# An eight-core kernel's first stage: seven of eight batches summed on TensorE, the eighth scaled on ScalarE, and two groups of instructions moved in their queues

## The chip, the cores and the metric

One Trainium2 chip, all 8 cores. Every core runs the same program on the same kind of data, with no exchange between them. The metric is the device time of the slowest core, in microseconds (us). A core has five engines with queues of their own, worked off in order: TensorE (PE, matmuls), VectorE (DVE), ScalarE (ACT), GpSimd (POOL) and SyncE (SP, which here issues transfers). They are held together only by semaphores.

## The reference

The program is a chain of four layers on x of 8 batches, 2048 tokens and 1024 features: a retention-like attention, a routed feed-forward, a delta-rule block and the routed feed-forward again. The change touches only the first one:

```python
def _L0_attn_a_ref(x, Wq, Wk, Wv):        # x: layer norm of the input
    Q = jnp.einsum('bti,id->btd', x, Wq)
    K = jnp.einsum('bti,id->btd', x, Wk)
    V = jnp.einsum('bti,id->btd', x, Wv)
    m = jnp.einsum('btd,bt->td', K, V.sum(axis=-1))
    ...
    return S[None, :, :] * Q              # S: decayed running sum of m over t
```

V's sum over its features is the product of the normed x with one vector, the row sums of Wv. So m is (sum over the 8 batches of c[b,t] * xhat[b,t,:]) times Wk, where c is a number per batch and token. The kernel works this out from the raw x: y = sum over b of coef[b,t] * x[b,t,:] plus a mean term, and then one product with Wk. Q is wanted for one batch only, the core's own (batch 0 of its data).

## The kernel before

**Tiles.** The tokens form NT = 16 tiles of 128. For each token tile `tt` there are B = 8 tiles of 128 tokens x 1024 features, f32, one a batch, numbered n = 8 tt + b. Four of them are a group gi (NGRP = 32 groups; group 2 tt has batches 0 to 3, group 2 tt + 1 has 4 to 7), and two are a unit (NUNIT = 64), which is what one transfer brings. They lie in `ring`, 16 slots, two token tiles deep.

**What each engine does in the first stage**, token tile by token tile:

- SP (L347 to L356) issues the units' transfers. Before it refills a slot it waits until PE has summed the old unit (`a_ymm`), and for a unit with batch 0 also until the own tile has been normed (`a_ownln`).
- ACT (`stats`, L401) takes sum and sum of squares of the tiles of six batches, three a group, in two passes each; `own_norm` (L417) makes the normed own tile `ownln`; `q_evict` (L428) copies Q from PSUM (`qps`) into `x_tok`. Order in a turn: `stats(2tt)`, `stats(2tt+1)`, `q_evict(tt-1)`, `own_norm(tt)`.
- DVE (`tiles`, L542) multiplies each tile by the vector of Wv's sums and adds up (`dotw`), and takes the statistics of batches 0 and 4; `coefs` (L557) makes four coefficients and signals `a_coef`; `mean_term` (L571); `own_evict` (L578) copies the transposed own tile to `ownfm`; `y_finish` (L584) adds the mean term to the sum in PSUM (`yps`) and writes `y16`; `y_evict` (L594) copies the transposed y to `y_fm`. Order in a turn: `tiles(2tt)`, `coefs(2tt)`, `own_evict(tt-1)`, `y_finish(tt-1)`, `tiles(2tt+1)`, `y_evict(tt-1)`, `coefs(2tt+1)`, `mean_term(tt)`.
- POOL (L368 to L375) makes, out of each coefficient column, a diagonal 128x128 matrix (`diag`, 8 places), and signals `a_diag` for each.
- PE (`y_rows`, L470) multiplies each tile by its diagonal, in two halves of 512 columns, and adds up the 8 batches in PSUM. An f32 product shows as two records in the trace, so a tile has four and a token tile 32. `own_project` (L483) first transposes `ownln` (8 small products, `trq`), waits for DVE's copy `ownfm`, and multiplies it by Wq (16 products, `qps`); `y_transpose` (L504) transposes `y16`. Order in a turn: `y_rows(2tt-1)`, `own_project(tt-1)`, `y_transpose(tt-1)`, `y_rows(2tt)`.

`yps` has two buffers, `qps` and the transposes' targets one each. The order on every engine is written out by hand. Behind the last Q product (`a_qmm` = 16) POOL loads Wk into the place of Wq, and PE multiplies y by it (L530): the second part of this layer. The rest of the program follows.

## Time and profile before

| | us |
|---|---|
| median of 3 runs (1994.53 to 1999.36) | 1994.77 |
| the profiled execution, slowest core | 1988.95 |
| its span (core 1, first to last instruction) | 1986.4 |
| spans of the eight cores | 1970.3 to 1986.4 |
| PE busy over the span | 1687.0 (85%) |
| DVE busy | 885.1 (45%) |
| ACT busy | 691.1 (35%) |
| POOL busy | 196.4 (10%) |

The rows below are of one execution and of its slowest core, core 1. Its first stage runs from the start to about 361 us. Times are from the core's first instruction. "Idle before" tells how long the engine had nothing to do ahead of a row, and what ended it. PE rows are merged runs of products; the end of the last one of a run is modelled, so the start-to-start time is the better measure.

### The profile page before, as it was taken

To read this page: it belongs to the slowest core of one execution; us is meant where nothing else is said; L and a number is where in the kernel's file an instruction comes from. 1 tells how busy PE (TensorE), PEld (TensorE's weight loads), DVE (VectorE), ACT (ScalarE), POOL (GpSimd) and SP (SyncE) were. 2 spreads that over 40 slices of the span, in tenths; PEclk is the share of its full clock that TensorE was granted. 3 is DMA by queue.
4 is the path that set the end of the run, shared out by engine and by line. 5 is a ranking of instruction groups with operands and counts; after the bars stand their busy time and mean duration, and the time that the engine had idled before them with its cause. 6 is when DMAs were issued, how large, how long until landed. Compare 5 with 4: busy or idle time off the path is not lost.

```text
span 1986.4 us, 23643 instructions; the slowest of 8 cores (1970.3 to 1986.4 us)
## 1 busy us (share of the span) xinstructions
PE 1687.0 (85%) x8330; PEld 801.6 (40%) x8330; DVE 885.1 (45%) x1699; ACT 691.1 (35%) x1051; POOL 196.4 (10%) x272
## 2 busy tenths in 40 slices
PE   1999999681399996898999999999999995289997
PEld 0444444230244442444554444444444442144443
DVE  3788888387421115436442432442222346611222
ACT  4788887047412223410323221340001110722112
POOL 2212121020301004000000000000000000300002
PEclk8999999895599997999999999999999998589999
DMA  9776773385227729920010010571044322173445
GB/s 277 217 233 203 221 217 123 66 147 105 86 43 128 127 53 205 246 48 1 1 44 22 22 43 1 104 135 27 1 70 85 58 43 53 43 233 64 85 85 85
DMA packets 69425, 201.14 MB, mean 101 GB/s; under 512 B 4606, under 2 KB 4670, under 8 KB 69312
## 3 DMA queue, kind: packets, MB, share of 16 engines
q0 software_dynamic: 40960, 94.76, 26.7%
q1 hardware_dynamic: 28352, 104.88, 16.5%
q8 instruction: 69, 1.13, 0.2%
q14 instruction: 44, 0.36, 0.1%
HBM read 228.97 MB, written 33.59 MB: 132 GB/s over the span
## 4 chain that ended last, share of the span: by engine, by line
PE 78%; DMA 7%; DVE 7%; issue 4%; ACT 2%; DVEq 1%; POOL 0%; ACTq 0%; another core or an unknown queue 0%; SPq 0%; POOLq 0%
PE v_h1ps L971 11%; PE v_h2ps L983 10%; PE yps L478 10%; PE mlp_a L1653 6%; PE mlp_a L1641 5%; PE ab_bank L1488 5%; PE ab_bank L1526 3%; PE mlp_a L1667 3%; PE ab_bank L1439 3%; PE mlp_r L1667 3%; PE ab_big L1413 3%; PE qps L499 3%; PE ab_bank L1432 3%; PE ab_bank L1382 3%; PE ab_bank L1501 2%
## 5 line engine op out<-in xcount | busy, mean ns | idle before, releaser
L478 PE MATMUL yps<-ring,diag 128*128 128x512 f32 x512 | 225.9, 599 | 12.1 <-POOL diag L374 12.1
L971 PE MATMUL v_h1ps<-m_sel_fm,m_w 128*128 128x512 bf16 x1024 | 222.5, 379 | 0.0
L983 PE MATMUL v_h2ps<-m_w,m_h1q 128*128 128x512 bf16 x1024 | 222.3, 379 | 0.0
L918 ACT ACTIVATE m_h1q<-v_h1ps,fb_s 128x512 bf16<-128x512 f32 x128 | 87.8, 687 | 294.4 <-PE v_h1ps L971 294.4
L891 DVE TENSOR_TENSOR m_acc<-v_h2ps,m_acc 128x512 f32<-128x512 f32 x96 | 66.3, 691 | 262.0 <-PE v_h2ps L983 262.0
L547 DVE SCALAR_TENSOR_TENSOR scr_v<-ring,wvs_bc 128x1024 bf16<-128x1024 f32 x128 | 152.6, 1211 | 0.6 <-issue 0.6
L971 PEld LDWEIGHTS v_h1ps<-m_sel_fm,m_w 128*128 128x128 bf16 x1024 | 100.3, 98 | 120.4 <-issue 0.3
L983 PEld LDWEIGHTS v_h2ps<-m_w,m_h1q 128*128 128x128 bf16 x1024 | 100.1, 98 | 120.9
L478 PEld LDWEIGHTS yps<-ring,diag 128*128 128x128 f32 x512 | 96.9, 192 | 128.8 <-issue 128.8
L1625 ACT ACTIVATE gate_prod<-mlp_a 128x512 bf16<-128x512 f32 x64 | 38.2, 597 | 273.8 <-PE mlp_a L1641 273.6
L1641 PE MATMUL mlp_a<-xln_fm,wg_buf 128*128 128x512 bf16 x512 | 113.8, 383 | 2.6 <-ACT gate_prod L1625 2.6
L1653 PE MATMUL mlp_a<-xln_fm,wu_buf 128*128 128x512 bf16 x512 | 111.8, 379 | 0.0
L413 ACT ACTIVATE scr_s<-ring,a_mv 128x1024 bf16<-128x1024 f32 x96 | 109.2, 1138 | 2.2
L1595 DVE TENSOR_TENSOR gate_prod<-mlp_a,gate_prod 128x512 bf16<-128x512 f32 x64 | 44.3, 692 | 135.7 <-PE mlp_a L1653 135.6
L408 ACT ACTIVATE scr_s<-ring 128x1024 bf16<-128x1024 f32 x96 | 100.3, 1046 | 7.2 <-DMA ring<-x_all 2.6
L374 POOL TENSOR_SCALAR diag<-cs_ident,a_coef 128x128 f32<-128x128 f32 x128 | 61.9, 501 | 249.2 <-DVE a_coef L567 244.1
L530 PE MATMUL mps<-y_fm,wk 128*128 128x512 bf16 x256 | 57.9, 387 | 26.7 <-DMA wk<-aWk 18.5
L1641 PEld LDWEIGHTS mlp_a<-xln_fm,wg_buf 128*128 128x128 bf16 x512 | 50.3, 99 | 64.8 <-issue 5.9
L1653 PEld LDWEIGHTS mlp_a<-xln_fm,wu_buf 128*128 128x128 bf16 x512 | 50.0, 98 | 60.2 <-issue 0.3
L1488 PE MATMUL ab_bank<-q_fm,k_fm 128*128 128x512 bf16 (+3 forms) x320 | 65.3, 347 | 9.5 <-DVE x_tok L1246 4.0
L499 PE MATMUL qps<-wq,ownfm 128*128 128x512 bf16 x256 | 57.8, 379 | 17.9 <-DVE ownfm L582 15.2
L1667 PE MATMUL mlp_a<-wd_buf,gate_prod 128*128 128x512 bf16 x256 | 60.4, 379 | 9.2 <-DVE gate_prod L1595 9.2
(263 smaller groups left out, 2251.4 us busy)
## 6 DMA issues: line engine op xcount, KB each, us to landing
ring<-x_all SPq DMA_DIRECT2D x64, 1024.0 KB, 6.8
m_w<-fW POOLq DMA_DIRECT2D x16, 2048.0 KB, 14.4
x_tok<-x_all POOLq DMA_DIRECT2D x16, 512.0 KB, 7.8
y_dram<-x_tok SPq DMA_DIRECT2D x4, 2048.0 KB, 26.6
x_tok<-y_dram SPq DMA_DIRECT2D x16, 512.0 KB, 4.4
x_tok<-y_dram POOLq DMA_DIRECT2D x16, 512.0 KB, 6.0
out<-x_tok SPq DMA_DIRECT2D x4, 2048.0 KB, 21.1
m_sel_tok<-sel_dram SPq DMA_DIRECT2D x8, 514.0 KB, 6.0
```

The lines of the kernel that those rows point to most:

```text
L408: s.activation(out=scr_s[:, q * D:(q + 1) * D], in_=x_tile(n), func=AF.Identity, scale=1.0 / (32.0 * D), accum_out=mv[:, 2 * n:2 * n + 1])
L413: ii = s.activation(out=scr_s[:, q * D:(q + 1) * D], in_=x_tile(n), func=AF.Square, scale=-1.0 / 32.0, bias=mv[:, 2 * n:2 * n + 1], accum_ ...
L478: ii = t.matmul(yps[tt % 2][:, h * 512:(h + 1) * 512], lhsT=diag_of(n), rhs=x_tile(n)[:, h * 512:(h + 1) * 512], start=(n % B == 0), stop= ...
L499: ii = t.matmul(qps[:, h * 512:(h + 1) * 512], lhsT=ownfm[:, dt * P:(dt + 1) * P], rhs=wq16[:, dt * D + h * 512:dt * D + (h + 1) * 512], s ...
L547: v.scalar_tensor_tensor(out=scr_v[:, j % 2 * D:(j % 2 + 1) * D], in0=x_tile(n), scalar=1.0, in1=wvs_bc[:, :], op0=ALU.mult, op1=ALU.mult, ...
L918: s.activation(out=h1q[:, ft * D + h * 512:ft * D + (h + 1) * 512], in_=h1ps[n % 4][:, :], func=AF.Gelu_apprx_tanh, bias=fb1_s[:, q * 8 + ...
L971: ii = t.matmul(h1ps[n % 4][:, :], lhsT=w1[:, dt * D + ft * P:dt * D + (ft + 1) * P], rhs=sel_fm[:, dt * D + h * 512:dt * D + (h + 1) * 51 ...
L983: ii = t.matmul(h2ps[m % 4][:, :], lhsT=h1q[:, ff * D + rt * P:ff * D + (rt + 1) * P], rhs=w2[:, ff * D + h * 512:ff * D + (h + 1) * 512], ...
L1488: ii = t.matmul(dst[:, lo:512], lhsT=fm_tile(k_fm, j, dt), rhs=fm_sb(src, I, dt, lo), start=dt == 0, stop=dt == ND - 1)
L1641: ii = t.matmul(psA[ft % 2][:, 0:512], lhsT=wg_buf[:, dt * D + ft * P:dt * D + (ft + 1) * P], rhs=xfm16[:, dt * T + tb * 512:dt * T + (tb ...
L1653: ii = t.matmul(psA[2 + ft % 2][:, 0:512], lhsT=wu_buf[:, dt * D + ft * P:dt * D + (ft + 1) * P], rhs=xfm16[:, dt * T + tb * 512:dt * T + ...
L1667: ii = t.matmul(dst, lhsT=prod_t[:, ff * 512 + ttl * P:ff * 512 + (ttl + 1) * P], rhs=wd_buf[:, ff * D + nh * 512:ff * D + (nh + 1) * 512] ...
```

## The change

PE sums only the first NPE = 7 batches of a token tile. The tile of the eighth is multiplied by its coefficient on ACT (`z_scale`), into a place of `x_tok` that is not in use yet (`z_of`: the last two token tiles' places in turn), and DVE's `y_finish` adds it while it adds the mean term. POOL makes seven diagonals a token tile instead of eight. The signals are counted anew (`diag_no`, `ymm_no`): there are still four `a_ymm` signals a token tile, the last one behind the single batch 6.

`own_project` is split: the transposes (`own_transpose(tt-1)`) stay behind `y_rows(2tt-1)`, the products with Wq and `y_transpose(tt-1)` go behind `y_rows(2tt)`. On ACT `q_evict` moves by a turn, to `q_evict(tt-2)` behind `stats(2tt)` and `z_scale(tt-1)`. On DVE `y_evict(tt-1)` goes behind `coefs(2tt+1)` and `mean_term(tt)`. SP's refill of a unit with batches 6 and 7 also waits for `a_z`, and the last two `q_evict` wait for `a_ysum`.

```diff
@@ -29,6 +29,8 @@
 NGRP = 2 * NT
 NUNIT = 4 * NT
 NSLOT = 8
+
+NPE = 7
 
 def build_consts():
     c = {}
...
@@ -335,6 +338,15 @@
         def unit_of(n):
             return n // 2
 
+        def z_of(tt):
+            return x_tok[:, (NT - 2 + tt % 2) * D:(NT - 1 + tt % 2) * D]
+
+        def diag_no(n):
+            return n // B * NPE + n % B + 1
+
+        def ymm_no(u):
+            return u // 4 * 4 + u % 4 + 1
+
         def diag_of(n):
             return diag[:, n % B * P:(n % B + 1) * P]
 
@@ -347,7 +359,9 @@
             for u in range(NUNIT):
                 if u >= NSLOT:
                     old = u - NSLOT
-                    s.wait_ge(sem('a_ymm'), at('a_ymm', old + 1))
+                    s.wait_ge(sem('a_ymm'), at('a_ymm', ymm_no(old)))
+                    if old % 4 == 3:
+                        s.wait_ge(sem('a_z'), at('a_z', old // 4 + 1))
                     if old % 4 == 0:
                         s.wait_ge(sem('a_ownln'), at('a_ownln', old // 4 + 1))
                 tt, bi = u // 4, 2 * (u % 4)
@@ -369,8 +383,10 @@
                 g.wait_ge(sem('a_coef'), at('a_coef', gi + 1))
                 for j in range(4):
                     n = 4 * gi + j
+                    if n % B >= NPE:
+                        continue
                     if gi >= 2 and j % 2 == 0:
-                        g.wait_ge(sem('a_ymm'), at('a_ymm', unit_of(n - B) + 1))
+                        g.wait_ge(sem('a_ymm'), at('a_ymm', ymm_no(unit_of(n - B))))
                     g.tensor_scalar(out=diag_of(n), in0=cS['ident32'][:, :], scalar1=coef[:, n:n + 1], scalar2=1.0,
                                     op0=ALU.mult, op1=ALU.mult).then_inc(sem('a_diag'), 1)
             g.wait_ge(sem('a_qmm'), at('a_qmm', NT))
@@ -425,8 +441,17 @@
                 s.activation(out=ownln[:, :], in_=x_tile(B * tt), func=AF.Identity, scale=orst[:, tt:tt + 1],
                              bias=onmr[:, tt:tt + 1]).then_inc(sem('a_ownln'), 1)
 
+            def z_scale(tt):
+                n = B * tt + NPE
+                s.wait_ge(sem('a_coef'), at('a_coef', 2 * tt + 2))
+                if tt >= 2:
+                    s.wait_ge(sem('a_ysum'), at('a_ysum', tt - 1))
+                s.activation(out=z_of(tt), in_=x_tile(n), func=AF.Identity, scale=coef[:, n:n + 1]).then_inc(sem('a_z'), 1)
+
             def q_evict(tt):
                 s.wait_ge(sem('a_qmm'), at('a_qmm', tt + 1))
+                if tt >= NT - 2:
+                    s.wait_ge(sem('a_ysum'), at('a_ysum', tt + 1))
                 for h in range(2):
                     ii = s.activation(out=x_tok[:, tt * D + h * 512:tt * D + (h + 1) * 512],
                                       in_=qps[:, h * 512:(h + 1) * 512], func=AF.Identity)
@@ -441,10 +466,14 @@
             ii.then_inc(sem('a_wvsum_s'), 1)
             for tt in range(NT):
                 stats(2 * tt)
+                if tt >= 1:
+                    z_scale(tt - 1)
+                if tt >= 2:
+                    q_evict(tt - 2)
                 stats(2 * tt + 1)
-                if tt >= 1:
-                    q_evict(tt - 1)
                 own_norm(tt)
+            z_scale(NT - 1)
+            q_evict(NT - 2)
             q_evict(NT - 1)
             for i in range(NT):
                 c, side = divmod(i, 2)
@@ -473,14 +502,16 @@
                     t.wait_ge(sem('a_ysum'), at('a_ysum', tt - 1))
                 for j in range(4):
                     n = 4 * gi + j
-                    t.wait_ge(sem('a_diag'), at('a_diag', n + 1))
+                    if n % B >= NPE:
+                        continue
+                    t.wait_ge(sem('a_diag'), at('a_diag', diag_no(n)))
                     for h in range(2):
                         ii = t.matmul(yps[tt % 2][:, h * 512:(h + 1) * 512], lhsT=diag_of(n),
-                                      rhs=x_tile(n)[:, h * 512:(h + 1) * 512], start=(n % B == 0), stop=(n % B == B - 1))
-                    if j % 2 == 1:
+                                      rhs=x_tile(n)[:, h * 512:(h + 1) * 512], start=(n % B == 0), stop=(n % B == NPE - 1))
+                    if j % 2 == 1 or n % B == NPE - 1:
                         ii.then_inc(sem('a_ymm'), 1)
 
-            def own_project(tt):
+            def own_transpose(tt):
                 t.wait_ge(sem('a_ownln'), at('a_ownln', tt + 1))
                 if tt >= 1:
                     t.wait_ge(sem('a_ownev'), at('a_ownev', tt))
@@ -488,6 +519,8 @@
                     ii = t.transpose(out=trq[:, dt * P:(dt + 1) * P], in_=ownln[:, dt * P:(dt + 1) * P],
                                      identity=cS['ident16'][:, :])
                 ii.then_inc(sem('a_owntr'), 1)
+
+            def own_project(tt):
                 if tt == 0:
                     t.wait_ge(sem('a_wq'), at('a_wq', 16))
                     t.wait_ge(sem('a_coef'), at('a_coef', 1))
@@ -513,10 +546,12 @@
             y_rows(0)
             for tt in range(1, NT):
                 y_rows(2 * tt - 1)
+                own_transpose(tt - 1)
+                y_rows(2 * tt)
                 own_project(tt - 1)
                 y_transpose(tt - 1)
-                y_rows(2 * tt)
             y_rows(2 * NT - 1)
+            own_transpose(NT - 1)
             own_project(NT - 1)
             y_transpose(NT - 1)
             t.wait_ge(sem('a_yev'), at('a_yev', NT))
@@ -582,13 +617,14 @@
                 v.tensor_copy(ownfm[:, :], trq[:, :]).then_inc(sem('a_ownev'), 1)
 
             def y_finish(tt):
-                v.wait_ge(sem('a_ymm'), at('a_ymm', 4 * (tt + 1)))
+                v.wait_ge(sem('a_ymm'), at('a_ymm', ymm_no(4 * tt + 3)))
+                v.wait_ge(sem('a_z'), at('a_z', tt + 1))
                 if tt >= 1:
                     v.wait_ge(sem('a_ytr'), at('a_ytr', tt))
                 v.drain()
                 for h in range(2):
-                    ii = v.tensor_scalar(out=y16[:, h * 512:(h + 1) * 512], in0=yps[tt % 2][:, h * 512:(h + 1) * 512],
-                                         scalar1=nbias[:, tt:tt + 1], scalar2=None, op0=ALU.add)
+                    ii = v.scalar_tensor_tensor(out=y16[:, h * 512:(h + 1) * 512], in0=yps[tt % 2][:, h * 512:(h + 1) * 512],
+                                                scalar=nbias[:, tt:tt + 1], in1=z_of(tt)[:, h * 512:(h + 1) * 512], op0=ALU.add, op1=ALU.add)
                 ii.then_inc(sem('a_ysum'), 1)
 
             def y_evict(tt):
@@ -617,10 +653,10 @@
                     own_evict(tt - 1)
                     y_finish(tt - 1)
                 tiles(2 * tt + 1)
+                coefs(2 * tt + 1)
+                mean_term(tt)
                 if tt >= 1:
                     y_evict(tt - 1)
-                coefs(2 * tt + 1)
-                mean_term(tt)
             own_evict(NT - 1)
             y_finish(NT - 1)
             y_evict(NT - 1)
```

## Rows read from the trace of the kernel before

**Rows 1.** The chain of waits in order of time, 40 to 420 us: start, us, what.

```profile
168.10 13.79 PE yps L478 x32
...
187.41 13.79 PE yps L478 x32
```

**Rows 2.** Timeline of PE: start, us, line, operation, count, [idle before <-releaser].

```profile
63.71 0.61 PE L488 MATMUL trq<-cs_ident,ownln 128*128 128x128 bf16 x8
67.00 3.61 PE L499 MATMUL qps<-wq,ownfm 128*128 128x512 bf16 x16 [2.68 <-DMA wq<-aWq]
...
70.89 13.95 PE L478 MATMUL yps<-ring,diag 128*128 128x512 f32 x32
84.68 0.61 PE L488 MATMUL trq<-cs_ident,ownln 128*128 128x128 bf16 x8
86.30 3.61 PE L499 MATMUL qps<-wq,ownfm 128*128 128x512 bf16 x16 [1.01 <-DVE ownfm L582]
89.75 0.61 PE L509 MATMUL try<-cs_ident,y 128*128 128x128 bf16 x8
...
97.55 7.11 PE L478 MATMUL yps<-ring,diag 128*128 128x512 f32 x16 [0.26 <-POOL diag L374]
```

**Rows 3.** Timeline of PE, the end of the stage.

```profile
341.26 0.61 PE L509 MATMUL try<-cs_ident,y 128*128 128x128 bf16 x8
341.71 13.95 PE L478 MATMUL yps<-ring,diag 128*128 128x512 f32 x32
...
357.12 3.61 PE L499 MATMUL qps<-wq,ownfm 128*128 128x512 bf16 x16 [1.01 <-DVE ownfm L582]
...
379.68 29.61 PE L530 MATMUL mps<-y_fm,wk 128*128 128x512 bf16 x128 [18.50 <-DMA wk<-aWk]
```

**Rows 4.** Timeline of ACT, one turn.

```profile
90.01 1.09 ACT L431 ACTIVATE x_tok<-qps 128x512 f32<-128x512 f32 x2 [2.53 <-PE qps L499]
90.99 0.20 ACT L419 ACTIVATE a_orst<-a_inv 128x1 f32<-128x1 f32 x1
...
93.05 1.06 ACT L408 ACTIVATE scr_s<-ring 128x1024 bf16<-128x1024 f32 x1
...
99.99 1.06 ACT L408 ACTIVATE scr_s<-ring 128x1024 bf16<-128x1024 f32 x1
```

**Rows 5.** Timeline of DVE, one turn.

```profile
72.79 0.69 DVE L596 COPY y_fm<-try 128x1024 bf16<-128x1024 bf16 x1
73.40 0.16 DVE L560 TENSOR_SCALAR a_inv<-a_mv 128x4 f32<-128x4 f32 x1
...
73.88 0.16 DVE L567 TENSOR_TENSOR a_coef<-a_dotw,a_inv 128x4 f32<-128x4 f32 x1
...
74.59 1.22 DVE L547 SCALAR_TENSOR_TENSOR scr_v<-ring,wvs_bc 128x1024 bf16<-128x1024 f32 x1
...
81.39 0.16 DVE L567 TENSOR_TENSOR a_coef<-a_dotw,a_inv 128x4 f32<-128x4 f32 x1
85.47 0.69 DVE L582 COPY ownfm<-trq 128x1024 bf16<-128x1024 bf16 x1 [3.91 <-PE trq L488]
86.25 1.41 DVE L590 TENSOR_SCALAR y<-yps,a_nbias 128x512 bf16<-128x512 f32 x2
87.58 1.22 DVE L547 SCALAR_TENSOR_TENSOR scr_v<-ring,wvs_bc 128x1024 bf16<-128x1024 f32 x1
```

**Rows 6.** Timeline of POOL; last row: the chain of waits, first diagonal of four.

```profile
74.27 2.46 POOL L374 TENSOR_SCALAR diag<-cs_ident,a_coef 128x128 f32<-128x128 f32 x4 [12.32 <-DVE a_coef L567]
81.79 1.41 POOL L374 TENSOR_SCALAR diag<-cs_ident,a_coef 128x128 f32<-128x128 f32 x4 [5.05 <-DVE a_coef L567]
...
96.07 1.34 POOL diag L374
```

**Rows 7.** Busy time by stretch: stretch, us, engines' busy (count), PEclk, DMA, GB/s.

```profile
415.00:420.00 5.00, 2.54 (x13) 1.01 (x12) 4.48 (x3) 2.39 (x4) 0.00 (x0) 1.00 0.88 163
...
425.00:430.00 5.00, 2.18 (x11) 0.83 (x10) 4.83 (x3) 1.77 (x3) 0.00 (x0) 1.00 1.03 204
```

More of the change, by code:

```diff
@@ L80 @@
     [('a_coef', 32), ('ab_pev', 64)],
-    [('a_diag', 128), ('ab_invT', 4)],
+    [('a_diag', 112), ('ab_invT', 4)],
     [('a_ymm', 64), ('ab_invTe', 4)],
+    [('a_z', 16)],
     [('a_ysum', 16), ('ab_invA', 24)],
```

## The prediction

> **What bounds the kernel now.** The pages of the cores come first: core 1 is the slowest, and all eight work alike, so I read core 1. Then the chain of waits in order of time: through the first stage it is a string of `yps` matmuls, the copy of `ownfm` and the `qps` matmuls, and it repeats every 187.41 - 168.10 = 19.31 us [rows 1]. TensorE (PE) is the bound. Its timeline splits the 19.31 us of one token tile: 32 matmul records for the sum over eight batches take 84.68 - 70.89 = 13.79 us (0.431 us each), from the own transposes to the Q products 1.62 us (of it 1.01 idle, waiting for the DVE copy), the Q products 3.45, the y transposes 0.45 [rows 2, 3]. The first tile has one more wait, 2.68 us for the load of Wq [rows 2]. The stage is over at 357.12 + 3.61 = 360.73 us, when the last Q product releases the load of Wk, for which PE then waits 18.50 us [rows 3]. So what counts is the time of the last Q product; everything later moves with it.
>
> The other engines are not far behind. ScalarE (ACT): two half tiles of statistics at 99.99 - 93.05 = 6.94 us, the Q eviction 0.98, the own norm 2.06, together 16.9 us [rows 4]. DVE: four tiles with their coefficients take 81.39 + 0.16 - 74.59 = 6.96 us, twice; `ownfm` 0.78, the finish of y 1.33, the mean term 0.5, the eviction of y 0.61, together 17.1 us [rows 5].
>
> **PE's work.** The eighth batch leaves PE: four records per tile, 4 x 0.431 = 1.72 us. The Q products now stand behind the next half sum, which covers the wait for `ownfm` (1.01 us, and 0.16 of latency) [rows 2]. PE's own work falls to 28 x 0.431 + 0.45 + 3.45 + 0.45 = 16.4 us. If PE stayed the bound, 2.9 us a tile would be won. It does not.
>
> **ACT's work.** The scaling of the eighth tile is one activation of 128x1024. It costs at least the 1.06 us of a statistics activation of that size and at most the 2.06 us of the whole own norm, which is such an activation behind two small ones [rows 4]; I take 1.2, nearer to the former. ACT's work rises to 18.1 us: that is the floor for any other ordering.
>
> **The new ring.** The order of the changed code has a loop that was not there before. In turn `tt` PE runs `y_rows(2tt)`, `own_project(tt-1)`, `y_transpose(tt-1)`. DVE's `y_evict(tt-1)` waits for that transpose, and it now stands behind `coefs(2tt+1)` and `mean_term(tt)`, last in its turn; queued behind it on DVE are `tiles(2tt+2)` and `coefs(2tt+2)`. Those coefficients feed GpSimd's (POOL's) diagonals, for which `y_rows(2tt+2)` waits. Once round is one tile, and nothing in it can overlap:
> - four batches on PE, 16 x 0.431 = 6.90 us [rows 2]
> - Q products 86.30 to 89.75, 3.45 us; eight transposes 0.61 us [rows 2]
> - signal from PE to DVE: the own transposes end at 84.68 + 0.61 = 85.29, DVE starts at 85.47, 0.18 us [rows 2, 5]
> - `y_evict`, start to start 73.40 - 72.79 = 0.61 us [rows 5]
> - four tiles and coefficients 6.96 us [rows 5]
> - coefficient to POOL: 73.88 + 0.16 to 74.27, 0.23 us [rows 5, 6]
> - the first diagonal: between 1.41 / 4 = 0.35 us, where DVE stood idle (81.79), and 1.34 us, where DVE was in its 128x1024 products (96.07) [rows 6]. Here DVE does the copy of `ownfm` from PSUM, not the product. I take 0.36; nothing suggests below 0.35
> - POOL to PE: 96.07 + 1.34 = 97.41 to 97.55, 0.14 us [rows 2, 6]
>
> The sum is 6.90 + 3.45 + 0.61 + 0.18 + 0.61 + 6.96 + 0.23 + 0.36 + 0.14 = 19.44 us, 0.13 us above the 19.31 of before. So the 2.9 us that PE gives up turn into a wait of PE for diagonals, 19.44 - 16.4 = 3.0 us in each tile, ahead of `y_rows(2tt)`. Before, `y_evict` stood in front of only the odd half's coefficients, and PE had 13.79 us of matmuls queued, so no such loop was tight.
>
> **What hides the rest.** With S for the start of `y_rows(2tt)` on PE: DVE ends `coefs(2tt)` at S - 0.73, then `ownfm` and the finish of y to about S + 1.5, four tiles, coefficients and mean by S + 9.0, and must wait for the transpose until S + 11.1. So the finish of y with its second operand, even if it took twice its 1.33 us, costs nothing. That finish also waits for the scaled tile: ACT makes it after `coefs(2tt-1)`, some 9 us ahead. ACT's chain from the Q products (S + 10.5) is eviction, 6.94, 2.06, 6.94, the scaling: by S + 29 it is ready for the next Q eviction, due at S + 30; cover about 1 us a tile. The Q eviction, two turns back in the code, is needed by PE only at S + 6.9 of the next turn. `y_rows(2tt+1)` needs its diagonals at S + 10.8 and they are there at about S + 9; if the odd first diagonal takes the 1.34 us, still so. SyncE's (SP's) refill of the unit with batches 6 and 7 now also waits for the scaling, and refills behind it queue; with 16 slots for 8 batches that scaling runs most of a tile before its slot is wanted. Two diagonals in sixteen less on POOL: its engine is idle most of the time, nothing. The last two Q evictions wait for the finish of y, because the scaled tile borrows their place: in the tail, under the 18.50 us of Wk [rows 3]. If one of these covers were missing, each 0.1 us would cost 1.4 us over the stage.
>
> **The ends.** This is where a little is won. The first `y_rows(2)` no longer waits for Q products and Wq. In the profiled execution the own transposes start at 63.71; with four records fewer at 61.99; S(1) = 61.99 + 0.45 = 62.44, against 70.89 now [rows 2]. Wq (67.0) is needed only at 69.3, so its 2.68 us go. From S(1) fourteen turns lead to S(15) = 62.44 + 14 x 19.44 = 334.60. From there to the last Q product: 6.90 + 3.45 + 0.45 + 12 x 0.431 + 1.62 + 3.61 = 21.20, so 355.80, against 360.73: **4.9 us earlier** [rows 2, 3]. The same count breaks even at (360.73 - 21.20 - 62.44) / 14 = 19.79 us a tile.
>
> The profiled execution took 1988.95 us, with a span of 1986.4; the median of the runs is 1994.77, 0.3% above it. Taking 4.9 us off either gives 1984.0 and 1989.9. I give **1989.9 us**, 0.25% less. The other cores' start of Q differs by some us, so their gains would be 3 to 8 us.
>
> **Rival 1, the first diagonal is slow (slower than before).** If POOL's first diagonal behind the even coefficients is held up by DVE's copy or by the new finish of y as the odd ones are by the products, it takes 1.34 us instead of 0.36 [rows 6]. T becomes 20.42: 14 x 0.98 = 13.7 us more, 8.8 us slower than before, 2003.6 us. It decides from a first diagonal of 0.36 + 0.35 = 0.71 us on. Against it: the slow ones coincide with products with two SBUF inputs, and here DVE reads PSUM. The Trainium skill, "SBUF — State Buffer", section "Who interferes with whom", says that a DVE instruction with two SBUF inputs shuts out a GpSimd one that reads SBUF, and that one with at most one SBUF input, outside the two-port modes, does not. By that rule, the trace's 1.34 us is explained and this rival doesn't happen; no row here shows a diagonal beside a copy from PSUM.
>
> **Rival 2, the ring isn't the bound.** If `y_evict` did not come last on DVE, ACT's 18.1 us would be the period: 14 x (18.1 - 19.44) = -18.8, with the ends -23.7, 1971.1 us. For it: it is what the engines' work alone gives. Against: all waits of the ring are in the code.
>
> **Rival 3, the clock falls.** PE idles 3.0 us in one piece per tile. After the 18.50 us idle of before, 128 records took 29.61 us where 128 x 0.216 = 27.6 would do at the high clock: 2.0 us a restart [rows 3]. At each tile that is 28 us, 23 us slower, 2018 us. Against it: with idle stretches of 2.5 to 2.8 us every 10 us, and PE busy 2.54 and 2.18 of 5 us, the granted clock was 1.00, the 2.4 GHz level [rows 7].
>
> **Chances.** A difference under 0.3% (6 us) can't be told from none. My forecast 0.70, of which 0.20 ends more than 6 us faster (a core with a later Wq is the slowest, or a turn 0.1 us shorter) and 0.50 within. Rival 1 0.18, of which 0.04 stays within 6 us; rival 2 0.06; rival 3 0.06. Faster 0.26, same 0.54, slower 0.20. The range reaches from 1984 (the forecast less 6 us for turns of 19.1 and the runs' spread) to 2004 (the upper bound of the first diagonal); outside are rivals 2 and 3 and a few per cent. The forecast's own range is 1985 to 1996.
>
> **What would show it.** In the changed profile: `y_rows(2tt)` starting every 19.4 us; PE idle near 3 us ahead of it, ended by POOL's `diag`; DVE idle near 2 us ahead of `y_fm`, ended by PE's `try`; no more wait of `qps` on `ownfm` or Wq; clock 1.00; last Q product near 356. A period near 18.1 with ACT without gaps shows rival 2; a first even diagonal of over 0.7 us rival 1. The prediction falls if the period is under 19.2 or over 19.8.

## The result, and the profile after

| | before | after |
|---|---|---|
| median of the undisturbed runs, slowest core, us | 1996.4 | 2023.76 |
| ratio of after to before | | 1.013 (95% interval 1.0079 to 1.0182) |
| profiled execution, us (its span) | 1988.95 (1986.4) | 2030.52 (2029.0) |
| start of the last Q product on PE, mean of the 8 cores, us | 359.2 | 369.4 |
| first K product to first V product of the delta block, mean, us | 79.0 | 86.8 |

The change makes the kernel 1.3% slower; I had said 0.25% faster, with 2004 us as the upper end. Some executions of every kernel here run with the clock of a whole die lowered; they are left out of all medians and ratios.

The cores of the changed kernel (span, mean granted clock):

```profile
core 0: 1997.8 us, clock 0.932
core 1: 1992.9 us, clock 0.935
...
core 4: 2029.0 us, clock 0.915
core 5: 2024.4 us, clock 0.919
```

Two things are to be seen: six cores end at 1993 to 2009 us, where the eight of before ended at 1970 to 1986, and cores 4 and 5 are another 15 to 36 us behind those six. So I read core 1, as before, for the stage, and core 4 for the rest.

PE's timeline of core 1, the first turns of the first stage (start, us, what, idle before):

```profile
62.41 7.08 PE L509 MATMUL yps<-ring,diag 128*128 128x512 f32 x16
69.33 3.62 PE L532 MATMUL qps<-wq,ownfm 128*128 128x512 bf16 x16
...
81.82 7.10 PE L509 MATMUL yps<-ring,diag 128*128 128x512 f32 x16 [2.77 <-POOL diag L390]
88.76 3.62 PE L532 MATMUL qps<-wq,ownfm 128*128 128x512 bf16 x16
92.22 0.61 PE L542 MATMUL try<-cs_ident,y 128*128 128x128 bf16 x8
...
101.25 8.54 PE L509 MATMUL yps<-ring,diag 128*128 128x512 f32 x16 [2.77 <-POOL diag L390]
109.62 3.62 PE L532 MATMUL qps<-wq,ownfm 128*128 128x512 bf16 x16
...
122.11 7.11 PE L509 MATMUL yps<-ring,diag 128*128 128x512 f32 x16 [2.78 <-POOL diag L390]
```

These answer to [rows 2]. The first `y_rows(2)` starts at 62.41 us (I had 62.44), the next at 81.82, the next at 101.25: 19.43 us a turn (I had 19.44), against the 19.31 of [rows 1]. PE waits 2.77 us for a diagonal in each (I had 3.0). But the sum that starts at 101.25 takes 8.54 us where the one at 81.82 took 7.10, though both have 16 records. Busy time and granted clock around it (stretch, us, busy of PE, PEld, DVE, ACT, POOL with counts, PEclk, DMA, GB/s):

```profile
101.00:110.00 9.00, 8.75 (x18) 3.85 (x19) 8.44 (x18) 8.23 (x15) 1.15 (x5) 0.83 0.62 191
110.00:119.00 9.00, 9.00 (x40) 4.33 (x39) 5.45 (x12) 6.53 (x11) 1.06 (x3) 1.00 0.52 186
```

From 101 to 110 us the mean clock was 0.83: for a part of it PE ran at its lower level, 1.2 GHz instead of 2.4. In front lies the 2.77 us wait. It is not so in every turn: the turn after it has 1.00 again, with the same wait ahead.

DVE and POOL of the same core, answering to [rows 5, 6]:

```profile
113.79 0.69 DVE L632 COPY y_fm<-try 128x1024 bf16<-128x1024 bf16 x1 [3.40 <-PE try L542]
...
121.21 0.16 DVE L602 TENSOR_TENSOR a_coef<-a_dotw,a_inv 128x4 f32<-128x4 f32 x1
121.60 0.69 DVE L617 COPY ownfm<-trq 128x1024 bf16<-128x1024 bf16 x1 [0.23 <-issue]
122.39 1.41 DVE L626 SCALAR_TENSOR_TENSOR y<-yps,a_nbias,x_tok 128x512 bf16<-128x512 f32 x2
123.72 1.22 DVE L582 SCALAR_TENSOR_TENSOR scr_v<-ring,wvs_bc 128x1024 bf16<-128x1024 f32 x1
```

```profile
121.60 1.41 POOL L390 TENSOR_SCALAR diag<-cs_ident,a_coef 128x128 f32<-128x128 f32 x4 [10.53 <-DVE a_coef L602]
```

The y eviction at 113.79 waited 3.40 us for PE's transposes; seven and a half microseconds later the coefficients are done (121.21 + 0.16), and PE's sum starts at 122.11. The four diagonals take 1.41 us beside DVE's copy of `ownfm`, 0.35 each. The finish of y with its second operand takes 123.72 - 122.39 = 1.33 us, as before. The sums of the waits from 80 to 360 us (us in total, times, longest):

```profile
DVE y_fm L632 <- PE try L542: 41.7, 14, 3.7
...
PE yps L509 <- POOL diag L390: 38.8, 14, 2.8
```

The end of the stage, answering to [rows 3]:

```profile
355.36 3.62 PE L532 MATMUL qps<-wq,ownfm 128*128 128x512 bf16 x16
...
366.09 3.61 PE L532 MATMUL qps<-wq,ownfm 128*128 128x512 bf16 x16 [1.01 <-DVE ownfm L617]
...
388.65 6.59 PE L565 MATMUL mps<-y_fm,wk 128*128 128x512 bf16 x17 [18.50 <-DMA wk<-aWk]
```

The last Q product ends at 366.09 + 3.61 = 369.70 us, against 360.73, and Wk is waited for the same 18.50 us.

### The profile page after: what moved, and what is told of

Its sections match the earlier page's. It is cut to its first block, busy times and chain, and to the rows that moved or that the text cites. A ratio compares the mean times of both kernels' runs of the same rounds, so it can differ in the third digit from the quotient of the medians.

```text
span 2029.0 us, 23413 instructions; the slowest of 8 cores (1992.9 to 2029.0 us)
## 1 busy us (share of the span) xinstructions
PE 1696.3 (84%) x8118; PEld 804.6 (40%) x8266; DVE 886.9 (44%) x1699; ACT 710.0 (35%) x1067; POOL 176.2 (9%) x256
## 3 DMA queue, kind: packets, MB, share of 16 engines
q8 instruction: 69, 1.13, 0.2%
## 4 chain that ended last, share of the span: by engine, by line
PE 73%; DVE 9%; DMA 7%; issue 5%; DVEq 3%; ACT 1%; POOL 1%; ACTq 0%; another core or an unknown queue 0%; SPq 0%; POOLq 0%
PE v_h1ps L1007 11%; PE v_h2ps L1019 10%; PE yps L509 7%; PE mlp_a L1689 5%; PE mlp_a L1677 5%; PE ab_bank L1524 5%; PE ab_big L1449 3%; PE ab_bank L1468 3%; PE ab_bank L1475 3%; PE qps L532 3%; PE mlp_a L1703 3%; PE ab_bank L1418 3%; PE mlp_r L1703 3%; PE ab_bank L1562 2%; PE ab_bank L1537 2%
## 5 line engine op out<-in xcount | busy, mean ns | idle before, releaser
L509 PE MATMUL yps<-ring,diag 128*128 128x512 f32 x448 | 214.7, 634 | 50.7 <-POOL diag L390 50.7
L509 PEld LDWEIGHTS yps<-ring,diag 128*128 128x128 f32 x448 | 88.6, 204 | 154.7 <-issue 154.7
L1468 PE MATMUL ab_bank<-x_tok,v_fm 128*128 128x512 bf16 x247 | 71.0, 438 | 0.8
L1418 PE MATMUL ab_bank<-h_fm,bwk 128*128 128x512 bf16 x248 | 66.3, 424 | 6.1 <-issue 3.7
```

Source lines behind the costliest of these rows:

```text
L509: ii = t.matmul(yps[tt % 2][:, h * 512:(h + 1) * 512], lhsT=diag_of(n), rhs=x_tile(n)[:, h * 512:(h + 1) * 512], start=(n % B == 0), stop= ...
L1418: ii = t.matmul(pj[n % 4][:, :], lhsT=bwk[:, dt * D + c * P:dt * D + (c + 1) * P], rhs=fm_sb(h_fm, sb, dt), start=dt == 0, stop=dt == ND - 1)
L1468: ii = t.matmul(pj[n % 4][:, :], lhsT=v_fm[:, dt * T + tt * P:dt * T + (tt + 1) * P], rhs=bwo[:, dt * D + h * 512:dt * D + (h + 1) * 512], ...
```

## The experiments

The columns of all PE rows below are those of above. "Last Q" is the start of the last single Q product, 0.4 us before it ends, as a mean of the eight cores; before has 359.2 and 361.0 in its two traces. Where no ratio is given, a kernel has only one or two undisturbed runs.

### The moves alone (e1_reorder_only)

The kernel before with the three moves; PE sums eight batches.

```diff
@@ PE
                 y_rows(2 * tt - 1)
-                own_project(tt - 1)
-                y_transpose(tt - 1)
+                own_transpose(tt - 1)
                 y_rows(2 * tt)
+                own_project(tt - 1)
+                y_transpose(tt - 1)
...
@@ DVE
-                if tt >= 1:
-                    y_evict(tt - 1)
                 coefs(2 * tt + 1)
                 mean_term(tt)
+                if tt >= 1:
+                    y_evict(tt - 1)
```

> The kernel before with the three moves alone (Q products behind the next half sum, Q eviction a turn later, y eviction behind the odd coefficients and the mean term); PE still sums all eight batches. Theory (the ring sets the period, and the clock that falls in PE's wait makes it longer): the ring of y_rows(2tt), Q products, y transposes, y eviction, four tiles, coefficients, diagonal is the same 19.4 us, but PE has 18.1 us of work in it, so it idles only 1.1 to 1.3 us a turn; the clock stays at its high level, period 19.4, last Q product 3 to 6 us earlier than before, whole kernel within 0.3% of before. Rival (the late first stage has another cause, the moves as such or the memory): period over 20 us here too, kernel 1% or more slower.

Ratio to before 0.9981 (0.9965 to 0.9997); last Q 357.6. Core 1:

```profile
100.11 7.11 PE L479 MATMUL yps<-ring,diag 128*128 128x512 f32 x16 [1.06 <-POOL diag L374]
...
119.54 7.10 PE L479 MATMUL yps<-ring,diag 128*128 128x512 f32 x16 [1.06 <-POOL diag L374]
```

The ring is there, 19.43 us, without the eighth batch having left PE; PE idles 1.06 us in it and no turn of fourteen is slow, on any of the eight cores. The ring costs next to nothing as long as PE has work to fill it. The rival (the moves as such) falls.

### PE's wait filled (e2_filler, e12_filler_6, e7_filler_3)

The changed kernel with products on PE that nobody reads, between the own transposes and the next half sum.

```diff
+            def warm(tt, count):
+                if tt < 2:
+                    return
+                t.wait_ge(sem('a_ysum'), at('a_ysum', tt - 1))
+                for k in range(count):
+                    t.matmul(yps[tt % 2][:, 0:512], lhsT=cS['ident16'][:, :], rhs=wq16[:, 0:512], start=True, stop=True)
...
                 own_transpose(tt - 1)
+                warm(tt, 11)          # 6 and 3 in the other two
                 y_rows(2 * tt)
```

> The changed kernel with 11 products of 128x512 (bf16, identity times a piece of Wq) on PE between the own transposes and y_rows(2tt), from turn 2 on, into the PSUM buffer that y_rows(2tt) then clears: about 2.4 us of work inside PE's 2.8 us wait. They change no result. Theory: the wait is no longer idle, the clock stays up, the four-batch sum takes 6.9 us in all turns instead of 8.4 to 8.7 in two of three; period 19.43 in all, last Q product about 13 us earlier than in the changed kernel, 3 to 5 us earlier than before; whole kernel near before (within 0.5%). Rival (the clock is a symptom or is lowered by something else): turns of 20.9 and 21.1 us remain, kernel 1% or more slower than before.

> The filler with 6 products: 1.3 us of work in PE's wait, so about 1.5 us idle a turn. At 1.06 us idle no turn lost its clock, at 2.1 and 2.8 us two of three did. If the length of the idle stretch alone decided, the losses here are as at 2.1 us or none; if they thin out with the length, one turn of three or fewer is 21.1 us. Last Q product 365 to 370 us if two of three, 360 to 364 if one of three, 354 to 356 if none.

> As the filler of 11 products, with 3 instead: 0.65 us of work in PE's wait, so that it idles about 2.1 us a turn. With 11 products (0.4 us idle) and in the kernel with the moves alone (1.06 us) no turn lost its clock, in the changed kernel (2.8 us) two of three did. Theory (the length of the idle stretch decides): either the clock holds, all turns 19.43 us and the last Q product 3 to 5 us earlier than before, or it falls in some turns, fewer than two of three, and each costs 1.4 to 1.7 us. It shows where between 1.1 and 2.8 us the loss begins. Rival (any product in the wait helps, its length doesn't matter): no turn is longer than 19.5 us.

With 11 products, undisturbed runs of 1991.0 and 1992.0 us; last Q 354.3, 15.1 us before the changed kernel's. With 6: 1994.62 us, last Q 354.7. With 3: 2008.09 us, last Q 369.6. Core 1, with 11, 6 and 3 products:

```profile
100.47 7.10 PE L509 MATMUL yps<-ring,diag 128*128 128x512 f32 x16 [0.40 <-POOL diag L390]
...
119.90 7.11 PE L509 MATMUL yps<-ring,diag 128*128 128x512 f32 x16 [0.40 <-POOL diag L390]
```

```profile
99.65 7.11 PE L509 MATMUL yps<-ring,diag 128*128 128x512 f32 x16 [1.48 <-POOL diag L390]
...
119.08 7.11 PE L509 MATMUL yps<-ring,diag 128*128 128x512 f32 x16 [1.48 <-POOL diag L390]
```

```profile
103.93 7.10 PE L509 MATMUL yps<-ring,diag 128*128 128x512 f32 x16 [2.13 <-POOL diag L390]
...
123.37 8.80 PE L509 MATMUL yps<-ring,diag 128*128 128x512 f32 x16 [2.13 <-POOL diag L390]
...
144.50 8.80 PE L509 MATMUL yps<-ring,diag 128*128 128x512 f32 x16 [2.13 <-POOL diag L390]
```

More work in PE's queue makes the stage 15 us shorter: the products cost nothing, and the clock holds. That is the cause of the late stage shown by itself. My estimate of 13 us was near. The idle stretch decides. Counted over the fourteen `y_rows(2tt)` from turn 2 on:

| kernel | PE idle ahead, us | sums over 8 us, core 1 | all cores |
|---|---|---|---|
| e2_filler | 0.40 | 0 of 14 | 0 of 112 |
| e3_evict_later (below) | 0.64 to 1.32 | 0 of 14 | 0 of 112 |
| e1_reorder_only | 1.06 | 0 of 14 | 0 of 112 |
| e12_filler_6 | 1.48 | 0 of 14 | 0 of 112 |
| e7_filler_3 | 2.13 | 9 of 14 | 69 of 112 |
| after | 2.77 | 9 of 14 | 78 of 112 |
| after, second trace (e5_after_again) | 2.77 | 11 of 14 | 80 of 112 |

The rival that any product would help falls with the 3 products. What was tested is the idle time in one piece; how busy PE is over the turn changes along with it.

### The ring opened (e3_evict_later), and closed further (e8_evict_back)

```diff
                 coefs(2 * tt)
+                if tt >= 2:
+                    y_evict(tt - 2)
                 if tt >= 1:
                     own_evict(tt - 1)
...
                 mean_term(tt)
-                if tt >= 1:
-                    y_evict(tt - 1)
+            y_evict(NT - 2)
```

> The changed kernel with DVE's y_evict(tt-1) taken one more step back, behind coefs(2tt+2) of the next turn, so that the tiles and coefficients no longer queue behind the wait for the y transposes. Theory: the ring is cut; ScalarE's work sets the period, 18.1 us, PE idles 1.5 to 1.8 us a turn in one or two pieces; last Q product 22 to 28 us earlier than before if the clock holds, kernel 1.0 to 1.4% faster than before. If the clock falls in this shorter wait too, 1.5 us a turn of it is lost, but ScalarE's floor hides part. Rival (the ring is not what holds the period): period stays over 19 us.

Undisturbed runs of 1962.7 and 1965.8 us; last Q 327.8, 31 us before that of the kernel before. Core 1:

```profile
95.20 7.11 PE L509 MATMUL yps<-ring,diag 128*128 128x512 f32 x16 [0.65 <-POOL diag L390]
...
112.50 7.10 PE L509 MATMUL yps<-ring,diag 128*128 128x512 f32 x16 [0.64 <-POOL diag L390]
```

```profile
PE yps L509 <- POOL diag L390: 10.6, 13, 1.3
...
DVE a_inv L595 <- ACT scr_s L429: 3.5, 6, 0.8
```

```profile
100.61 1.24 ACT L441 ACTIVATE ownln<-ring,a_onmr,a_orst 128x1024 bf16<-128x1024 f32 x1
...
118.32 1.24 ACT L441 ACTIVATE ownln<-ring,a_onmr,a_orst 128x1024 bf16<-128x1024 f32 x1
```

The period is 112.50 - 95.20 = 17.30 us here, 17.6 to 18.0 from about 215 us on, and 17.5 in the mean of the fourteen turns. One DVE instruction, moved behind the next turn's even coefficients, was worth (369.4 - 327.8) / 14 = 3.0 us a turn against the changed kernel: 1.9 from the period, 1.0 from the clock, which no longer falls. The rival falls. It also shows a number of mine wrong: I had 18.1 us as ScalarE's floor. Its own norm comes every 118.32 - 100.61 = 17.71 us, on all eight cores, with no idle stretch over 0.42 us in its queue from 90 to 310 us: that is its floor. The half tile's statistics take 6.7 us in front of the scaling or the own norm, not the 6.94 between two halves, which held one more drain of the queue, and the scaling itself 1.04 to 1.13. At first DVE sets the turn (on core 1 17.30 us, with no wait of its own over 0.2 us), and ScalarE falls 0.4 us a turn behind; then DVE waits for ScalarE's statistics, in six turns, and ScalarE sets it.

In e8 the eviction goes back to its old place, ahead of the odd coefficients, the rest as changed.

> The changed kernel with the y eviction back where it was before, ahead of the odd coefficients and the mean term, the rest as changed. Theory (the ring): the wait for the y transposes now stands ahead of the odd coefficients and the mean term as well, so that these 1.19 us join the ring: period 19.43 + 1.19 - 0.1 = 20.5 us at the high clock, PE idle 3.9 to 4.1 us a turn, and the clock falls in at least as many turns as in the changed kernel: 1.4 to 1.7 us more in each. Last Q product 22 to 35 us later than before. Rival (the eviction's move made the ring): period 19.3 us or less.

2018.57 us; last Q 374.6. Core 1:

```profile
102.38 7.11 PE L509 MATMUL yps<-ring,diag 128*128 128x512 f32 x16 [1.68 <-POOL diag L390]
...
115.49 5.39 PE L509 MATMUL yps<-ring,diag 128*128 128x512 f32 x12 [2.11 <-POOL diag L390]
...
123.00 7.11 PE L509 MATMUL yps<-ring,diag 128*128 128x512 f32 x16 [1.67 <-POOL diag L390]
...
197.97 7.08 PE L509 MATMUL yps<-ring,diag 128*128 128x512 f32 x12 [2.11 <-POOL diag L390]
205.48 7.10 PE L509 MATMUL yps<-ring,diag 128*128 128x512 f32 x16
```

The period is 123.00 - 102.38 = 20.62 us, where the sum of the ring said 20.5. But PE's wait now lies in two pieces, 2.11 and 1.68 us, and not in one of 4 as I had expected, and the last Q product is 13.6 to 15.4 us later than before rather than 22 to 35. The clock does fall: behind the 2.11 us the twelve records of the odd half sum take 7.08 us instead of 5.39 in 60 of 112 turns of the eight cores (core 1 from 198 us on; granted clock 0.81 from 197 to 206 us). But the odd half sum is not in the ring. The 1.69 us go into the wait behind it, which is then gone (205.48), and the turn stays at 20.62. So in this stage a fall of the clock costs time where the work it slows is in the ring, and here nothing.

### One part each (e4_seven_only, e11_evict_move_only)

e4 has the eighth batch on ScalarE and every queue in the order of before:

```diff
                 y_rows(2 * tt - 1)
-                own_transpose(tt - 1)
+                own_project(tt - 1)          # with the transposes in it again
+                y_transpose(tt - 1)
                 y_rows(2 * tt)
-                own_project(tt - 1)
-                y_transpose(tt - 1)
...
-                if tt >= 2:
-                    q_evict(tt - 2)
                 stats(2 * tt + 1)
+                if tt >= 1:
+                    q_evict(tt - 1)
                 own_norm(tt)
```

> The changed kernel's first part alone: seven batches on PE, the eighth scaled on ScalarE, with all queues in the order of before (Q products and y transposes behind y_rows(2tt-1), Q eviction behind stats(2tt+1), y eviction ahead of the odd coefficients). Theory: no ring of 19.4 us; PE has 17.6 us with its wait for the DVE copy, ScalarE 18.1: period about 18.1 us, last Q product 14 x 1.2 + 1.7 = 18 to 20 us earlier than before, kernel 0.8 to 1.1% faster than before. Rival (the scaling on ScalarE or the second operand of the finish costs more than its rows say): period 18.8 us or more, kernel within 0.5% of before or slower.

Ratio 0.9912 (0.9879 to 0.9945); last Q 334.6. Core 1:

```profile
102.77 3.61 PE L532 MATMUL qps<-wq,ownfm 128*128 128x512 bf16 x16 [1.01 <-DVE ownfm L615]
...
120.36 3.61 PE L532 MATMUL qps<-wq,ownfm 128*128 128x512 bf16 x16 [1.01 <-DVE ownfm L615]
```

120.36 - 102.77 = 17.59 us: PE is the bound with its 17.6, not ScalarE with 18.1 as I had expected, and the last Q product comes 24.6 us earlier than in the first trace of before instead of 18 to 20. ScalarE's 17.70 us a turn, again with no idle stretch over 0.42 us, are 0.1 more than PE's; it falls behind by that much in each turn, and the stage is over before anyone waits long for it. So the first part alone is a gain of 0.9%, and it is the moves on top of it that turn it into a loss.

e11 has the eviction's move alone, on the kernel before.

> The kernel before with one edit: the y eviction behind the odd coefficients and the mean term, Q products and y transposes where they were, all eight batches on PE. Theory (the ring needs both moves: y transposes behind the next half sum, and the eviction ahead of the next tiles): the transposes come 6.9 us earlier in the turn, so the eviction never waits for them, and PE's queue sets the period as before, 19.31 us; last Q product within 1 us of before. Rival (the eviction's place alone lengthens the turn): period over 19.4 us.

1996.98 us; last Q 360.8; slowest core:

```profile
90.90 13.95 PE L478 MATMUL yps<-ring,diag 128*128 128x512 f32 x32
...
110.21 13.95 PE L478 MATMUL yps<-ring,diag 128*128 128x512 f32 x32
```

19.31 us as before: the eviction's place does no harm by itself. The ring needs both, the y transposes behind the next half sum and the eviction behind the coefficients.

### Behind the stage (e5_after_again, e6_before_again, e10_after_pad, e9_evict_later_pad)

Second traces of the changed kernel and of the kernel before:

> The changed kernel once more, beside the kernel before on the same chip. Its last Q product came 10 us later than before (mean of the cores), its slowest core 27 us later. Theory: the first stage gives 10 us in every run (turns of 19.4, 21.1 and 20.9 us, of which the last two have a clock that fell), and the rest lies behind the stage and is not of the change: with new runs the median core is 12 to 16 us later than before, and the slowest core 12 to 25. Rival: a second effect of the change behind the stage, present in all runs: then the median core too is 20 us later or more.

> The kernel before once more, for a second trace of it: how long the parts behind the first stage take on each core. The first trace has 1620 us (mean of the cores) from the last Q product to the end, where the four experiments so far have 1627 to 1632 and the changed kernel 1636. If the first trace was a lucky one, this has 1625 to 1630, and the changed kernel's excess behind the stage shrinks to 6 to 11 us; if it is typical, 1618 to 1622 again.

e5 had one undisturbed run, 2028.92 us, with a median core of 2002.4 (the four of the result have 1999.2 to 2002.1; eleven of before have a median of 1986.2). e6: 2002.03 us. From the last Q product to the end, mean of the cores: before 1620.2 and 1626.8, after 1636.3 and 1636.1. So my first trace of before was on the lucky side, and an excess of 9 to 16 us behind the stage remains. It came again in the second trace of the changed kernel, so my theory that it is not of the change falls. In parts:

| mean of the cores, us | before, twice | e1 | e11 | e2 | e7 | e3 | e4 | e8 | after, twice |
|---|---|---|---|---|---|---|---|---|---|
| first K to first V product | 79.0, 80.6 | 80.6 | 82.2 | 82.5 | 84.4 | 85.8 | 85.0 | 86.6 | 86.8, 86.5 |
| of it PE idle, released by nothing | 0.1, 0.1 | 0.1 | 0.1 | 0.8 | 2.9 | 3.1 | 3.6 | 3.5 | 3.8, 3.6 |
| product records on PE less those of before | 0 | 0 | 0 | +90 | -22 | -64 | -64 | -64 | -64 |

In a stage the change doesn't touch, PE stands still at one place of its queue. Core 1 of the changed kernel, in the last K products:

```profile
854.56 0.61 PE L1418 MATMUL ab_bank<-h_fm,bwk 128*128 128x512 bf16 x2
858.98 14.98 PE L1418 MATMUL ab_bank<-h_fm,bwk 128*128 128x512 bf16 x62 [3.82 <-issue]
```

The two products ahead of the gap and the next six are one loop of eight without a wait between them. In the changed kernel, e3, e4, e5 and e8 all eight cores stand there, 62 product records before the first V product, whatever the time. With 3 filler products (e7) five cores stand, and with 11 (e2) two cores (4.8 and 1.5 us, hence the mean of 0.8), both in 128 small products that also have no wait between them. Core 1 of e7:

```profile
857.16 2.24 PE L1440 MATMUL ab_bank<-ab_bt,h_fm 128*128 128x1 bf16 x84
863.44 1.33 PE L1440 MATMUL ab_bank<-ab_bt,h_fm 128*128 128x1 bf16 x44 [4.04 <-issue]
```

That is 110 records before the first V product in e7 and 94 in e2: the place moves when products are added ahead of it. The stand comes in kernels with another number of products in the first stage than before. e10 and e9 put as many back, small ones, where PE waits for Wk anyway:

```diff
             t.wait_ge(sem('a_qev'), at('a_qev', NT))
+            for k in range(4 * NT):
+                t.matmul(mps[0][:, 0:64], lhsT=cS['ident16'][:, :], rhs=cS['ident16'][:, 0:64], start=True, stop=True)
             t.wait_ge(sem('a_wk'), at('a_wk', 16))
```

> The changed kernel with the same 64 small products in PE's wait for Wk. Theory: the stand inside the K products goes here too, 4 to 6 us off the stretch behind it; the first stage stays as it was (last Q product near 370 us). Median core 1993 to 1997, that is 8 to 11 us later than before, all of it from the first stage. If also the two cores of a pair that so far ran at a granted clock of 0.81 from about 870 us on (22 us longer than the others) run like the others, the slowest core is 10 to 14 us later than before; if not, that pair is not tied to the stand. Rival: nothing changes behind the first stage.

> The kernel with the y eviction one more step back (last Q product 31 us earlier than before, but only 24 to 28 us of that left at the end), and 64 small products of 64 columns on PE in its wait for Wk, as many product records as the sum over seven batches has fewer. They touch nothing that is read. In the traces so far PE stands for 2.9 to 3.8 us (mean of the cores) without any releaser inside the K products of the delta block in every kernel with seven batches and 64 or 22 records fewer on PE, 0.8 us with 90 more, and 0.1 us with as many as before. Theory (PE's instruction stream is refilled at a place counted in instructions, and in seven-batch kernels that place falls into the transfers of Wq and Wo): with the count restored the stand is 0.1 to 0.3 us, the stretch from the first K product to the first V product takes 79 to 82 us instead of 86, and the kernel is 1.6 to 2.0% faster than before. Rival (the stretch is longer because the cores come to it at other times): still 85 us or more, and the stand remains.

e10, the changed kernel: ratio 1.0048 (1.0029 to 1.0066) instead of 1.013, each to the kernel before beside it. The stand is 0.1 us, the stretch 79.4, the last Q product 370.5 as expected. The same place on core 1:

```profile
856.60 15.67 PE L1420 MATMUL ab_bank<-h_fm,bwk 128*128 128x512 bf16 x64
```

e9, the opened ring: ratio 0.9832 (0.9808 to 0.9857), the best version here, 1.7% faster than before; stand 0.1, stretch 81.1. The filler with 6 products, 20 records more than before, fits too (0.1 and 81.3).

The third part of the excess sits on two cores. Core 4 and core 1 of the changed kernel (columns as above):

```profile
880.00:940.00 60.00, 59.65 (x226) 24.80 (x228) 27.81 (x7) 0.48 (x1) 0.00 (x0) 0.81 0.00 1
```

```profile
880.00:940.00 60.00, 58.25 (x365) 30.05 (x362) 41.62 (x47) 0.00 (x0) 0.00 (x0) 1.00 0.00 1
```

Core 4 had a granted clock of 0.81 all through the V products; its neighbour 5 as well, until 1033 us. It costs them 12 us in the V products (67.0 against 55.0) and 10 to 12 in the next part, 22 in all. In e5 it was cores 2 and 3. In one more run of the changed kernel, without a trace, cores 6 and 7 stand out in the same way (2028.5 and 2023.1 us, mean clocks 0.916 and 0.919). In these three the pair makes the slowest core; the other two undisturbed runs, with slowest cores at 2015.9 and 2006.9 us, show no such pair. The eight of e10 have theirs at 2003 to 2009, so no run with the count restored shows a pair. What ties the pair to the change is not shown. The stand alone doesn't do it: in e3, e4, e7 and e8 it is 2.9 to 3.6 us long, and all eight cores take 55 us for the V products. e10 ran on another chip than e5, and lowered clocks on several cores come with the kernel before too.

## Why the prediction was wrong

**What bounds the kernel:** right. PE set the period of before; a little less work on PE alone (e4) shortened the turn to PE's new 17.59 us.

**The new ring:** right. 19.43 us was measured for 19.44, S(1) = 62.41 for 62.44, the diagonals 0.35 beside the copy. Of the terms only the signal from PE to DVE is off by more than 0.04 us: 92.22 + 0.61 to 92.93, 0.10 us for 0.18. With the clock up, in e2, the last Q product came 4.9 and 6.7 us earlier than in the two traces of before, for 4.9.

**Rival 1**, the slow first diagonal: did not happen. By the rule of the Trainium skill, "SBUF — State Buffer", "Who interferes with whom", a DVE instruction with at most one SBUF input, outside the two-port modes, does not contend with GpSimd. The trace agrees: beside DVE's copy from PSUM the four diagonals took 1.41 us.

**Rival 2**, the ring isn't the bound: false for this code, but its floor was also 0.4 us too high (17.7 in e3 and e4 for 18.1): two `stats` durations of 6.94 us, each with a drain of the queue more than the 6.7 that they take there, and 1.2 us for a scaling of 1.04 to 1.13; the Q eviction behind it took 1.19 us rather than 0.98.

**Rival 3**, the clock, is the step that failed. I gave it 0.06 and it happened. Core 1 has nine slow turns, four at 1.69 us and five at 1.43 more than 19.43: 13.9 us. My 355.80 plus 13.9 is the 369.70 of the trace. My price, 2.0 us in all fourteen turns, 28 us, was twice that; the chance was wrong by more. The argument against it was [rows 7]: a clock of 1.00 on core 1 beside waits of 2.5 and 2.8 us. That was one core and two windows. The same execution of the kernel before, in the same products on cores 7 and 5, shows the fall behind the same 2.46 us:

```profile
411.12 8.75 PE L530 MATMUL mps<-y_fm,wk 128*128 128x512 bf16 x32 [2.46 <-DVE s_fm L641]
```

```profile
420.38 7.07 PE L530 MATMUL mps<-y_fm,wk 128*128 128x512 bf16 x32 [2.46 <-DVE s_fm L641]
...
439.79 8.67 PE L530 MATMUL mps<-y_fm,wk 128*128 128x512 bf16 x32 [2.46 <-DVE s_fm L641]
```

7.07 us is 32 products at the full clock; 8.75 and 8.67 are the same 1.6 to 1.7 us that the changed kernel then lost nine times on core 1. In the first trace of before, PE waited 2.46 us or longer in these products twenty times on the eight cores, and five of the runs of products behind it were slow, each on another core, by 1.6 us in the mean. Those rows, read before predicting, would have put the clock into the sum, as an estimate at 14 x 5/20 x 1.6 = 5.6 us, which makes 1989.9 + 5.6 = 1995.5 us. That is still 8 us short of the 13.9: they show that it falls behind such a wait, and not how often it does in this stage.

**Behind the stage:** I had it that everything later moves with the last Q product. It didn't: 6.9 us more in the K products (of them 3.6 the stand; the other 3.3 went too when e10 restored the count, and why is open), and in three of five runs 22 us on one pair of cores. No row of before shows either. For the median core, with the means of both pairs of traces, the sum is 9.8 (the last Q product) + 6.9 = 16.7 us, measured 14.6 (2000.8 against 1986.2); for the slowest core it is mostly the pair on top of that which makes the 27. The range left this out altogether; e10, where only the first stage differs, has a ratio of 1.0048, which on the 1994.77 of before is 2004.3 us: 14 us over the forecast, at the range's upper end.

## What to carry to other kernels

Before an instruction that waits is moved back in a queue, walk once round from it: which engine's work stands behind it, what that work feeds, and whether that comes back to the instruction's own release within one turn; such a ring has a period of its own, and the cure is to move the wait past the work that feeds the ring (here 17.5 us in the mean instead of 19.43). Work taken off TensorE is only a gain if TensorE doesn't then wait; where it does, look for its clock in the rows of all cores behind waits of that length, and price it. And when a change shortens an engine's instruction stream, look once over the stages behind it for a stand without a releaser.

## What the hardware showed that I had not expected

- Idle stretches of PE of 0.4 to 1.48 us, once a turn, never cost its clock in the first stage (448 turns on the eight cores of four kernels); 2.13 and 2.77 us cost it in 69 to 80 turns of 112, mostly two turns lost and one kept, 1.4 to 1.7 us each (once 3.0 on core 1 of e5). Where the slowed work was not in the ring (e8) the turn was no longer for it. Eleven products without a use, 2.4 us, bought 15 us.
- A run of products without waits stood still for 2.9 to 3.8 us (mean of the cores) when the stream ahead of it was 22 or 64 product records shorter, 0.8 us when 90 longer, and not when it was equal or 20 longer. It lies in transfers that keep the DMA engines busy (DMA share 0.94 to 1.01 from 790 to 860 us on the eight cores of the changed kernel). That the instruction stream's refill is late there is my reading: no row shows a refill. The Trainium skill, "Runtime: NRT & Kernel Launch", "Instruction fetch mechanics", says that the sequencer fetches its stream in blocks over its own DMA queue, mostly hidden; if the reading is right, the trace has a block's edge that is not hidden, for 3.8 us. What speaks for it is that the stand's place moves with the count: 48 records earlier with 42 records more ahead of it (e7 against after), 32 earlier with 154 more (e2). Edges every 128 products would give 49 and 33, with each product counted together with its weight load, and each added wait as half of one; the 128 is an estimate that fits these two shifts. Why an edge elsewhere in the stream (before, e10, e12) shows no stand is open.
- A pair of cores ran at a granted clock of 0.81 for some 160 us in both traces of the changed kernel; the spans of a third undisturbed run of five look the same, and none of eight with 64 small products added 500 us earlier. What ties the two, if anything does, is open.
